# Masked query copies of an attention kernel divided between GpSimd and VectorE

## The chip, the cores and the metric

The kernel runs on one core of a Trainium2 chip. The metric is device time in microseconds (us) of one execution. The engines are named as the profile names them: PE (TensorE; PEld its weight loads), DVE (VectorE), ACT (ScalarE), POOL (GpSimd), SP (SyncE, which issues the loads and stores here). SBUF and PSUM are the two on-chip memories; DVE and ACT read both, POOL works on SBUF here.

## What is computed

For 2048 samples of 40 fields with 64 features, four heads of 32:

```python
q = (einsum('bfe,oe->bfo', x, Wq) + bq).reshape(B, F, H, D)
k = (einsum('bfe,oe->bfo', x, Wk) + bk).reshape(B, F, H, D)
v = (einsum('bfe,oe->bfo', x, Wv) + bv).reshape(B, F, H, D)
att = softmax(einsum('bfhd,bghd->bhfg', q, k) / sqrt(64), axis=-1)
out = einsum('bhfg,bghd->bfhd', att, v).reshape(B, F, H * D)
y = relu(out + einsum('bfe,oe->bfo', x, Wr) + br)
```

## The kernel before

The 2048 samples are done in 256 steps of 8 samples (320 tokens). The steps are pipelined by hand: each engine has one loop over n, and in the loop's group n it works on several steps at once. Engines meet only through counting semaphores, and each engine runs its own instructions in the order in which they are written.

PE, group n: queries and keys of step n (L386, L390, into the two halves of the PSUM tile `o_bank`), scores of step n-1 (L406, into `s_buf`), attention times values of step n-3 (L475, into `o_bank` again), the shift of the scores by their maxima of step n-2 (L452), values and residual of step n (L422 to L438, into `vr_bank`). Since `o_bank` is shared, L386 of step n waits until DVE has divided the result of step n-4 (semaphore `att_ready` at n - 3), and L475 waits until ACT and DVE have copied queries and keys out (`copied`).

DVE, group n: combine and split the maxima of step n-2 (L331, L332, L336, out `m_split`), copy the keys of step n out of PSUM (L320, `kT`), reduce the scores of step n-1 to maxima (L325), and for step n-3 the reciprocal of the sums (L341) and the division (L347, out `y_att`).

ACT, group n: copy the queries of step n out of PSUM (L231, `q_flat`), values and residual (L258), swap maxima (L244), exponentials (L251), relu (L238).

POOL, group n: for step n-2 the diagonal matrices that PE's shift multiplies with (L183, `m_diag`, waits for `m_split`), for step n the masked copies of the queries (L199, `q_bd`), and for step n-4 the sum with the residual (L191, `y_sum`).

The masked copies are needed because 64 rows of `q_flat` hold a pair of heads. `q_bd[:, step, sample, s]` is a copy of the queries in which the rows of the pair's other head are multiplied by 0 and those of head s by 1, so that one matmul of 64 rows gives the scores of both heads, 80 columns. Copy s is one `tensor_scalar` of 128 x 320 fp32 elements, from contiguous `q_flat` in SBUF to `q_bd` in SBUF in 8 rows of 40 elements 80 apart, with a per-partition factor from `consts`. POOL makes both, one after the other. `q_ready` counts them: PE waits for two per step ahead of L390, and ACT before it writes `q_flat`'s buffer again, two steps on.

Of the kernel before, what the change touches and what calls it, by code (L numbers as in the profile page):

```python
# [6 lines left out]
ALU = mybir.AluOpType  # L7
# [27 lines left out]
def attention_kernel(nc, xT_in, w_in, bias_in, vr_bias_in, const_in, out):  # L35
# [3 lines left out]
    with ExitStack() as ctx:  # L39
# [3 lines left out]
        def sem(name):  # L43
            return ctx.enter_context(nc.semaphore(name))
# [47 lines left out]
        qk_made = sem("qk_made")  # L92
        copied = sem("copied")
        q_ready = sem("q_ready")
        scores_made = sem("scores_made")
        vr_made = sem("vr_made")
        vr_ready = sem("vr_ready")
# [24 lines left out]
        def before(n, limit):  # L122
            return n < limit
# [53 lines left out]
        @block.gpsimd  # L177
        def _(pool):
            def diagonals(n, place):
                pool.wait_ge(m_ready, 2 * (n + 1))  # L180
                if not before(n, 1):
                    pool.wait_ge(shifted, n)
                pool.tensor_tensor(m_diag[:], m_split[:, place % 2].unsqueeze(2).to_broadcast([P, BLOCKS, QUAD]),  # L183
                                   ident[:].unsqueeze(1).to_broadcast([P, BLOCKS, QUAD]),
                                   ALU.mult).then_inc(diag_ready, 1)

            def add_residual(n, place):
                pool.wait_ge(att_ready, n + 1)
                if not before(n, 3):
                    pool.wait_ge(y_ready, n - 2)  # L190
                pool.tensor_tensor(y_sum[:, n % 3].rearrange("r (a d) -> r a d", d=DIM), rv[:, place % 4, RESIDUAL * HEADS:(RESIDUAL + SLOTS) * HEADS, 0:DIM],  # L191
                                   y_att[:, place % 2].rearrange("r (a d) -> r a d", d=DIM),
                                   ALU.add).then_inc(sum_ready, 1)

            def query_columns(n, place):
                pool.wait_ge(copied, 2 * (n + 1))

                for s in range(2):
                    pool.tensor_scalar(q_bd[:, place % 4, :, s], q_flat[:, place % 2].rearrange("d (b f) -> d b f", f=FIELDS),  # L199
                                       consts[:, C_HEAD + s:C_HEAD + s + 1], 1.0, ALU.mult, ALU.mult).then_inc(q_ready, 1)  # L200

            def group(n, place):
                if not before(n, 2):
                    diagonals(n - 2, place + 6)
                query_columns(n, place)
                if not before(n, 4):
                    add_residual(n - 4, place + 4)

            pool.wait_ge(prepared, PREPARED)
            pool.wait_ge(set_up, SET_UP)  # L210
            run(group)
            for n in range(STEPS, STEPS + 4):
                if exists(n - 2):
                    diagonals(n - 2, n - 2)
                add_residual(n - 4, n - 4)

        @block.scalar
        def _(act):
            act.dma_start(consts[:], const_in).then_inc(loaded, 16)
            act.dma_start(vr_bias[:], vr_bias_in.to_broadcast([P, 2, OUT])).then_inc(loaded, 16)  # L220
            act.dma_start(biases[:], bias_in).then_inc(loaded, 16)
            act.wait_ge(loaded, LOADS)
            for i in range(4):
                nc.scalar.copy(rv[:, i, :, DIM:VW],
                               consts[:, C_REAL:C_REAL + 1].unsqueeze(2).to_broadcast([P, 2 * SLOTS * HEADS, 1])).then_inc(prepared, 1)

            def queries(n, place):
                act.wait_ge(qk_made, n + 1)
                if not before(n, 2):
                    act.wait_ge(q_ready, 2 * (n - 1))  # L230
                nc.scalar.activation(q_flat[:, place % 2], o_bank[:, 0, 0:TOK], ACT.Identity,  # L231
                                     bias=biases[:, 0:1]).then_inc(copied, 1)

            def relu(n, place):
                if not before(n, 4):
                    act.wait_ge(y_stored[place % 4], 32 * (turn_of(n, place, 4) - 1))
                act.wait_ge(sum_ready, n + 1)
                nc.scalar.activation(y_rows[:, place % 4], y_sum[:, n % 3], ACT.Relu).then_inc(y_ready, 1)  # L238

            def swap_maxima(n, place):  # L240
                act.wait_ge(m_parted, n + 1)
                for g in range(0, P // QUAD, 2):
                    to, of = QUAD * g, QUAD * (g + 1)
                    nc.scalar.copy(m_swap[to:to + QUAD, place % 2], m_part[place % 2][of:of + QUAD]).then_inc(m_swapped, 1)  # L244

            def exponentials(n, place):
                act.wait_ge(shifted, n + 1)
                if not before(n, 2):

                    act.wait_ge(o_made, n - 1)  # L250
                nc.scalar.activation(pT[:, place % 2], s_buf[place % 2][:, :, 0:TOK], ACT.Exp,  # L251
                                     scale=SCALE).then_inc(p_ready, 1)

            def values_and_residual(n, place):
                act.wait_ge(vr_made, n + 1)
                if not before(n, 4):
                    act.wait_ge(sum_ready, n - 3)
                nc.scalar.activation(rv[:, place % 4, :, 0:DIM],  # L258
                                     vr_bank[:].rearrange("k t (a d) -> k (t a) d", d=DIM),
                                     ACT.Copy).then_inc(vr_ready, 1)  # L260

            act.wait_ge(prepared, PREPARED)

            def group(n, place):
                queries(n, place)
                if not before(n, 1):
                    values_and_residual(n - 1, place + 7)
                if not before(n, 1):
                    swap_maxima(n - 1, place + 7)
                if not before(n, 2):  # L270
                    exponentials(n - 2, place + 6)
                if not before(n, 5):
                    relu(n - 5, place + 3)

            run(group)
            for n in range(STEPS, STEPS + 5):
                if exists(n - 1):
                    values_and_residual(n - 1, n - 1)
                    swap_maxima(n - 1, n - 1)
                if exists(n - 2):  # L280
                    exponentials(n - 2, n - 2)
                relu(n - 5, n - 5)

        @block.vector
        def _(dve):
# [32 lines left out]
            def keys(n, place):  # L318
                dve.wait_ge(qk_made, n + 1)
                nc.vector.tensor_scalar(kT[:, place % 4], o_bank[:, 1, 0:TOK], biases[:, 1:2], None,  # L320
                                        ALU.add).then_inc(copied, 1)

            def max_of_quadrants(n, place):
                dve.wait_ge(scores_made, n + 1)
                nc.vector.tensor_reduce(m_part[place % 2].rearrange("k (t b) -> k t b", t=2),  # L325
                                        s_buf[place % 2][:, :, 0:TOK].rearrange("k t (b c) -> k t b c", c=QUAD),
                                        AX.X, ALU.max, apply_transpose=True).then_inc(m_parted, 1)
# [24 lines left out]
            def group(n, place):  # L352
                if not before(n, 2):
                    max_of_keys(n - 2, place + 6)
                keys(n, place)
                if not before(n, 1):
                    max_of_quadrants(n - 1, place + 7)
                if not before(n, 3):
                    normalise(n - 3, place + 5)
                    divide(n - 3, place + 5)  # L360
# [11 lines left out]
        def _(pe):  # L372
# [5 lines left out]
            def queries_and_keys(n, place):  # L378
                if n == 0:
                    pe.wait_ge(x_loaded[0], 32)  # L380
                elif before(n, LAG + 1):
                    pe.wait_ge(copied, 2 * n)
                else:

                    pe.wait_ge(att_ready, n - LAG)
                nc.tensor.matmul(o_bank[:, 0, 0:TOK], w_cols[0:HALF, 0], tokens(place, 0), start=True, stop=True)  # L386
                if n > 0:

                    pe.wait_ge(q_ready, 2 * n)
                nc.tensor.matmul(o_bank[:, 1, 0:TOK], w_cols[HALF:P, 0], tokens(place, HALF),  # L390
                                 start=True, stop=True).then_inc(qk_made, 1)

            def scores(n, place):
# [2 lines left out]
                if not before(n, 2):  # L396
                    pe.wait_ge(p_ready, n - 1)
                if not exists(n + 1):
                    pe.wait_ge(q_ready, 2 * (n + 1))
                for slot in range(SLOTS):  # L400
                    for member in range(MEMBERS):
                        b = MEMBERS * slot + member
# [145 lines left out]
```

## Time and profile before

| | before |
|---|---|
| median of 3 runs | 927.33 us (925.72 to 928.43) |
| the profiled execution, whole | 923.84 us |
| span of its instructions | 921.1 us |
| granted TensorE clock, mean | 0.996 |
| PE busy | 892.3 us (97%) |
| POOL busy | 872.1 us (95%) |
| ACT busy | 770.6 us (84%) |
| DVE busy | 726.7 us (79%) |

The terms of the prediction are durations from the one profiled execution. The 2.7 us between its time and its span are start and end. Busy times are sums over a span whose steady part is 256 like steps; what bounds a step is read from the order of instructions in one step and from who waits for whom.

### The profile page before, as it was taken

The page shows a single profiled execution, that of the slowest core. Times are in us where ns is not written, and L with a number is a line of the kernel's source. Part 1 is how long each engine was busy: PE and PEld are TensorE (multiplying, and loading weights), DVE is VectorE, ACT ScalarE, POOL GpSimd, SP SyncE. Part 2 cuts the span into 40 slices and gives each one's busy share as a digit, 9 for nine tenths or more (in the row PEclk, how much of TensorE's full clock was granted, in tenths as well). Part 3 has the DMA queues.
Part 4 walks back from the last instruction along what each step waited for, and adds up shares of the span by engine and source line. Part 5 has one row for each costly group of instructions (what it writes and reads, how often), then busy time and mean ns, then how long its engine had stood idle before and what let it go on. Part 6 is the DMA issues. An engine that isn't in the chain of part 4 may idle for free.

```text
span 921.1 us, 67888 instructions
## 1 busy us (share of the span) xinstructions
PE 892.3 (97%) x30208; PEld 626.7 (68%) x30208; DVE 726.7 (79%) x2066; ACT 770.6 (84%) x1541; POOL 872.1 (95%) x1028
## 2 busy tenths in 40 slices
PE   6999999999999999999999999999999999999996
PEld 4667666767666776676666667666667766767664
DVE  5878777878787877888887878787878887878785
ACT  4888888888888888888888888888888888888886
POOL 3999999999999999999999999999999999999997
PEclk9999999999999999999999999999999999999998
DMA  4333333333333333333333333333333333333321
GB/s 120 97 110 117 113 105 110 115 107 112 118 112 107 116 111 111 111 117 109 115 112 105 110 111 111 112 112 112 117 111 112 112 120 108 115 110 112 111 83 67
DMA packets 67429, 101.20 MB, mean 110 GB/s; under 512 B 13632, under 2 KB 46656, under 8 KB 67136
## 3 DMA queue, kind: packets, MB, share of 16 engines
q1 hardware_dynamic: 66704, 96.72, 34.7%
q8 instruction: 235, 3.85, 1.8%
q14 instruction: 58, 0.48, 0.2%
q10 hardware_dynamic: 432, 0.15, 0.1%
HBM read 54.88 MB, written 41.94 MB: 105 GB/s over the span
## 4 chain that ended last, share of the span: by engine, by line
PE 93%; POOL 3%; issue 2%; DVE 1%; DMA 0%; ACT 0%; POOLq 0%; ACTq 0%
PE vr_bank L422 24%; PE o_bank L475 22%; PE s_buf L406 19%; PE o_bank L386 15%; PE s_buf L452 7%; PE vr_bank L433 6%; POOL y_sum L191 1%; POOL m_diag L183 1%; POOL q_bd L199 1%; PE o_bank L390 0%; DMA biases<-bias_in 0%; ACT y_rows L238 0%; POOLq L39 0%; DVE s_buf L325 0%; PE vr_bank L438 0%
## 5 line engine op out<-in xcount | busy, mean ns | idle before, releaser
L183 POOL TENSOR_TENSOR m_diag<-m_split,ident 128x640 bf16<-128x640 bf16 x256 | 323.1, 1262 | 32.2 <-DVE m_split L336 30.1
L191 POOL TENSOR_TENSOR y_sum<-rv,y_att 128x512 f32<-128x512 f32 x256 | 303.9, 1187 | 1.9 <-DVE y_att L347 1.9
L199 POOL TENSOR_SCALAR q_bd<-q_flat,consts 128x320 f32<-128x320 f32 x512 | 267.6, 537 | 11.2 <-DVE kT L320 11.1
L422 PE MATMUL vr_bank<-w_cols,xT 64*128 64x128 f32 (+1 forms) x3072 | 269.0, 308 | 0.1
L258 ACT ACTIVATE rv<-vr_bank 128x1024 f32<-128x1024 f32 x256 | 260.4, 1017 | 0.1
L325 DVE TRANSPOSE_TENSOR_REDUCE s_buf<-s_buf 128x20 f32<-128x640 f32 x256 | 221.6, 866 | 47.8 <-PE s_buf L406 47.7
L475 PE MATMUL o_bank<-rv,pT 64*40 64x33 f32 x16384 | 229.6, 202 | 12.1 <-issue 8.4
L406 PEld LDWEIGHTS s_buf<-q_bd,kT 64*40 64x40 f32 x8192 | 151.5, 113 | 116.2 <-issue 115.1
L475 PEld LDWEIGHTS o_bank<-rv,pT 64*40 64x40 f32 x16384 | 192.9, 117 | 54.4 <-issue 17.9
L320 DVE TENSOR_SCALAR kT<-o_bank,biases 128x320 f32<-128x320 f32 x256 | 140.9, 550 | 89.1 <-PE o_bank L390 89.0
L406 PE MATMUL s_buf<-q_bd,kT 64*40 64x80 f32 x8192 | 200.5, 233 | 1.4 <-issue 1.1
L422 PEld LDWEIGHTS vr_bank<-w_cols,xT 64*128 64x128 f32 x3072 | 195.2, 190 | 0.2 <-issue 0.2
L231 ACT ACTIVATE q_flat<-o_bank,biases 128x320 f32<-128x320 f32 x256 | 135.1, 528 | 71.5 <-PE o_bank L390 66.9
L386 PE MATMUL o_bank<-xT,w_cols 64*128 64x320 f32 x512 | 186.8, 445 | 5.7 <-DMA xT<-xT_in 5.7
L251 ACT ACTIVATE pT<-s_buf 128x640 f32<-128x640 f32 x256 | 180.4, 705 | 14.1 <-PE s_buf L452 8.0
L390 PE MATMUL o_bank<-xT,w_cols 64*128 64x320 f32 x512 | 187.5, 446 | 0.0
L347 DVE TENSOR_TENSOR y_att<-o_bank,r_sum 128x512 f32<-128x512 f32 x256 | 177.0, 691 | 9.2 <-DVE r_sum L341 0.3
L238 ACT ACTIVATE y_rows<-y_sum 128x512 f32<-128x512 f32 x256 | 159.1, 622 | 2.5 <-POOL y_sum L191 2.4
L244 ACT COPY m_swap<-s_buf 32x20 f32<-32x20 f32 x512 | 85.9, 168 | 55.5 <-DVE s_buf L325 49.4
L452 PE MATMUL s_buf<-m_diag,pick 64*40 64x320 bf16 x1024 | 114.9, 297 | 2.0 <-POOL m_diag L183 1.6
L386 PEld LDWEIGHTS o_bank<-xT,w_cols 64*128 64x128 f32 x512 | 76.6, 186 | 45.7 <-DVE y_att L347 35.4
L336 DVE TENSOR_TENSOR m_split<-s_buf,m_split 32x20 bf16<-32x20 f32 x512 | 88.5, 173 | 16.6
(31 smaller groups left out, 466.0 us busy)
## 6 DMA issues: line engine op xcount, KB each, us to landing
xT<-xT_in SPq DMA_DIRECT2D x512, 104.0 KB, 2.7
y<-y_rows SPq DMA_DIRECT2D x512, 80.0 KB
w_cols<-w_in SPq DMA_DIRECT2D x1, 192.0 KB, 2.6
vr_bias<-vr_bias_in ACTq DMA_DIRECT2D x1, 128.0 KB, 3.3
consts<-consts_in ACTq DMA_DIRECT2D x1, 20.0 KB, 2.4
biases<-bias_in ACTq DMA_DIRECT2D x1, 1.0 KB, 3.8
```

The costliest lines, as they stand in the source:

```text
L183: pool.tensor_tensor(m_diag[:], m_split[:, place % 2].unsqueeze(2).to_broadcast([P, BLOCKS, QUAD]), ident[:].unsqueeze(1).to_broadcast([P, ...
L191: pool.tensor_tensor(y_sum[:, n % 3].rearrange("r (a d) -> r a d", d=DIM), rv[:, place % 4, RESIDUAL * HEADS:(RESIDUAL + SLOTS) * HEADS, 0 ...
L199: pool.tensor_scalar(q_bd[:, place % 4, :, s], q_flat[:, place % 2].rearrange("d (b f) -> d b f", f=FIELDS), consts[:, C_HEAD + s:C_HEAD + ...
L251: nc.scalar.activation(pT[:, place % 2], s_buf[place % 2][:, :, 0:TOK], ACT.Exp, scale=SCALE).then_inc(p_ready, 1)
L258: nc.scalar.activation(rv[:, place % 4, :, 0:DIM], vr_bank[:].rearrange("k t (a d) -> k (t a) d", d=DIM), ACT.Copy).then_inc(vr_ready, 1)
L325: nc.vector.tensor_reduce(m_part[place % 2].rearrange("k (t b) -> k t b", t=2), s_buf[place % 2][:, :, 0:TOK].rearrange("k t (b c) -> k t ...
L386: nc.tensor.matmul(o_bank[:, 0, 0:TOK], w_cols[0:HALF, 0], tokens(place, 0), start=True, stop=True)
L390: nc.tensor.matmul(o_bank[:, 1, 0:TOK], w_cols[HALF:P, 0], tokens(place, HALF), start=True, stop=True).then_inc(qk_made, 1)
L406: mm = nc.tensor.matmul(s_buf[place % 2][HALF * member:HALF * member + FIELDS, t, 2 * FIELDS * slot:2 * FIELDS * (slot + 1)], kT[rows, pla ...
L422: return nc.tensor.matmul(blocks(half, first, step)[:, 0:count], xT[rows, place % 8, PAIR * pair:PAIR * pair + P], w_cols[rows, 1:1 + coun ...
L452: mm = nc.tensor.matmul(s_buf[place % 2][HALF * member:HALF * member + FIELDS, t, 0:TOK], pick[rows, member, 0:FIELDS], m_diag[rows, t * ( ...
L475: mm = nc.tensor.matmul(o_part[HALF * g:HALF * g + FIELDS, c, idx * HEADS + h], pT[HALF * member:HALF * (member + 1), place % 2, h // 2, a ...
```

## The change

In each step POOL writes the copy of the first head only (s = 0); the copy of the second head (s = 1) becomes a DVE instruction of the same form, written behind the keys' copy L320 and ahead of the maxima L325. DVE waits for `copied` (the queries by ACT and the keys by itself) ahead of it, and counts it on a semaphore of its own, `q_second`. PE waits for `q_second` in the first steps and in the last; in between it is covered by `att_ready`, which the same engine raises later. ACT's wait before it overwrites `q_flat` now counts POOL's copies alone.

```diff
+        q_second = sem("q_second")
...
             def query_columns(n, place):
                 pool.wait_ge(copied, 2 * (n + 1))
 
-                for s in range(2):
-                    pool.tensor_scalar(q_bd[:, place % 4, :, s], q_flat[:, place % 2].rearrange("d (b f) -> d b f", f=FIELDS),
-                                       consts[:, C_HEAD + s:C_HEAD + s + 1], 1.0, ALU.mult, ALU.mult).then_inc(q_ready, 1)
+                pool.tensor_scalar(q_bd[:, place % 4, :, 0], q_flat[:, place % 2].rearrange("d (b f) -> d b f", f=FIELDS),
+                                   consts[:, C_HEAD:C_HEAD + 1], 1.0, ALU.mult, ALU.mult).then_inc(q_ready, 1)
...
-                    act.wait_ge(q_ready, 2 * (n - 1))
+                    act.wait_ge(q_ready, n - 1)
...
+            def query_columns(n, place):
+                dve.wait_ge(copied, 2 * (n + 1))
+                nc.vector.tensor_scalar(q_bd[:, place % 4, :, 1], q_flat[:, place % 2].rearrange("d (b f) -> d b f", f=FIELDS),
+                                        consts[:, C_HEAD + 1:C_HEAD + 2], 1.0, ALU.mult, ALU.mult).then_inc(q_second, 1)
+
...
                 keys(n, place)
+                query_columns(n, place)
                 if not before(n, 1):
                     max_of_quadrants(n - 1, place + 7)
...
                     pe.wait_ge(copied, 2 * n)
+                    pe.wait_ge(q_second, n)
...
-                    pe.wait_ge(q_ready, 2 * n)
+                    pe.wait_ge(q_ready, n)
...
-                    pe.wait_ge(q_ready, 2 * (n + 1))
+                    pe.wait_ge(q_ready, n + 1)
+                    pe.wait_ge(q_second, n + 1)
```

## Rows read from the trace of the kernel before

**Rows 1.** The page: the span and each engine's busy time

```profile
span 921.1 us, 67888 instructions
...
PE 892.3 (97%) x30208; PEld 626.7 (68%) x30208; DVE 726.7 (79%) x2066; ACT 770.6 (84%) x1541; POOL 872.1 (95%) x1028
```

**Rows 2.** Waits: who waited for whom, us in total, times, longest us

```profile
DVE s_buf L325 <- PE s_buf L406: 47.7, 255, 0.8
...
PEld o_bank L386 <- DVE y_att L347: 35.4, 214, 0.3
...
POOL m_diag L183 <- DVE m_split L336: 30.1, 91, 1.6
...
PEld s_buf L452 <- POOL m_diag L183: 1.9, 2, 1.0
...
PE s_buf L452 <- POOL m_diag L183: 1.6, 2, 0.9
```

**Rows 3.** Timeline of a short step: start us, us, engine, line, [idle before it]

```profile
433.64 0.45 PE L386 MATMUL o_bank<-xT,w_cols 64*128 64x320 f32 x1
...
434.16 1.26 POOL L183 TENSOR_TENSOR m_diag<-m_split,ident 128x640 bf16<-128x640 bf16 x1
...
434.41 0.53 ACT L231 ACTIVATE q_flat<-o_bank,biases 128x320 f32<-128x320 f32 x1
434.41 0.55 DVE L320 TENSOR_SCALAR kT<-o_bank,biases 128x320 f32<-128x320 f32 x1 [0.33 <-PE o_bank L390]
...
435.13 0.87 DVE L325 TRANSPOSE_TENSOR_REDUCE s_buf<-s_buf 128x20 f32<-128x640 f32 x1 [0.16 <-PE s_buf L406]
435.40 1.04 POOL L199 TENSOR_SCALAR q_bd<-q_flat,consts 128x320 f32<-128x320 f32 x2
...
435.90 0.26 DVE L341 RECIPROCAL r_sum<-o_bank 128x16 f32<-128x16 f32 x1
...
436.19 0.69 DVE L347 TENSOR_TENSOR y_att<-o_bank,r_sum 128x512 f32<-128x512 f32 x1
436.40 1.19 POOL L191 TENSOR_TENSOR y_sum<-rv,y_att 128x512 f32<-128x512 f32 x1
...
436.94 0.18 PEld L386 LDWEIGHTS o_bank<-xT,w_cols 64*128 64x128 f32 x1 [0.15 <-DVE y_att L347]
...
437.03 0.45 PE L386 MATMUL o_bank<-xT,w_cols 64*128 64x320 f32 x1
...
437.09 0.38 DVE L336 TENSOR_TENSOR m_split<-s_buf,m_split 32x20 bf16<-32x20 f32 x2
...
437.55 1.26 POOL L183 TENSOR_TENSOR m_diag<-m_split,ident 128x640 bf16<-128x640 bf16 x1
...
437.80 0.55 DVE L320 TENSOR_SCALAR kT<-o_bank,biases 128x320 f32<-128x320 f32 x1 [0.33 <-PE o_bank L390]
```

**Rows 4.** Timeline of a long step, same columns

```profile
457.96 0.44 PE L386 MATMUL o_bank<-xT,w_cols 64*128 64x320 f32 x1
...
458.47 1.26 POOL L183 TENSOR_TENSOR m_diag<-m_split,ident 128x640 bf16<-128x640 bf16 x1 [0.23 <-DVE m_split L336]
...
460.48 0.26 DVE L341 RECIPROCAL r_sum<-o_bank 128x16 f32<-128x16 f32 x1 [0.18 <-PE o_bank L475]
...
461.59 0.46 PE L386 MATMUL o_bank<-xT,w_cols 64*128 64x320 f32 x1
```

**Rows 5.** Line L320: count, ns min/median/max, first and last start

```profile
L320 DVE TENSOR_SCALAR kT<-o_bank,biases x256: 546/550/553, 8.4 to 904.9; 128x320 f32<-128x320 f32 x128
```

**Rows 6.** Groups by line and form: single instructions of the set-up, busy us, mean ns

```profile
L293 DVE TENSOR_TENSOR out_bias<-vr_bias 128x128 f32<-128x128 f32 x1 | 0.3, 293 | 1.9 <-DMA biases<-bias_in 1.9
...
L295 DVE CAST bias_high<-out_bias 128x128 bf16<-128x128 f32 x1 | 0.2, 226 | 0.0
...
L311 DVE CAST ident<-consts 128x32 bf16<-128x32 f32 x1 | 0.2, 176 | 0.0
```

**Rows 7.** Timeline of POOL at the start: its first instruction on data

```profile
9.21 1.04 POOL L199 TENSOR_SCALAR q_bd<-q_flat,consts 128x320 f32<-128x320 f32 x2 [8.77 <-DVE kT L320]
```

## The prediction

> **What bounds the kernel now.** I read the page first: PE is busy 97% of the span and POOL 95%, DVE only 79% [rows 1]. That looks like PE and POOL being the limits and DVE having room, which is the case for moving work from POOL to DVE. The waits are read next, and they say something else: of 255 steps, in 214 PE's first weight load of a step (L386) is released by DVE's division L347, while PE waited for POOL's `m_diag` twice, for 1.9 and 1.6 us in sum [rows 2]. So the third view is the timeline of one short step. Taking PE's L386 at 433.64 as zero: DVE copies the keys from 0.77 to 1.32, waits 0.16 for PE's scores, reduces from 1.49 to 2.36, takes the reciprocal from 2.26, divides from 2.55 to 3.24, PE loads the next step's weights at 3.30 and multiplies at 3.39 [rows 3]. From there DVE waits for PE's keys, and the ring closes. Length 3.39 us. Of this ring DVE's own instructions are all but the stretch from the division's end to the next L320 (0.92 us, in which L331 to L336 run) and the 0.16.
>
> POOL's ring is as long: from `m_diag` to `m_diag` 434.16 to 437.55, again 3.39 us, in pieces of 1.24, 1.00 (both copies) and 1.15 us, without a gap [rows 3]. But POOL does not set the step: in the short step `m_diag` starts 0.08 us after `m_split` ends (437.09 + 0.38 = 437.47), and in the long step too it is `m_split` that ends POOL's wait, at 0.51 us after L386 against 0.52 in the short one [rows 3, 4]. `m_diag` stands at this place whether POOL had been idle or not.
>
> Not all steps are short. L320 starts at 8.4 for the first and at 904.9 for the last step: 896.5 / 255 = 3.516 us each [rows 5], 0.126 over 3.39, 32 us in all. The long steps (3.63 in the example) have their delay in the attention matmuls: L341 starts at 2.52 after L386 instead of 2.26, waiting for L475 [rows 3, 4]. POOL's waits count them: 91, with 30.1 us [rows 2], 0.33 each. This matters below, since a longer DVE part hides such delays.
>
> **The change part by part.** *POOL loses one copy of two*: 1.00 / 2 = 0.50 us per step, 128 us in all. Gain on the path: nothing, since `m_diag` starts by `m_split`. An upper bound is the 3.5 us that PE waited for it [rows 2]. The first head's copy keeps its place at 435.40 and ends 0.5 earlier than the pair did; PE needs it only at 437.03 (L386 and L390 of the next step).
>
> *DVE gains a copy of 128 x 320 fp32 per step*, in SBUF on both sides; no such instruction is in the trace. Its duration by the nearest rows: `kT` of the same size and form, but from PSUM, takes 0.550 us [rows 5]. One element takes DVE 1.04 ns at the single pace (a fp32 `tensor_tensor` of 512 elements 0.69 us, one of 128 elements 0.293 [rows 3, 6]), so that is 0.333 us for 320 elements and 0.217 fixed. The casts from fp32 in SBUF to SBUF take 226 ns for 128 elements and 176 for 32 [rows 6]: 50 ns for 96, 0.52 ns each, so two elements in the time of one, and 0.159 fixed. Copy at the doubled pace: 0.167 + 0.217 = 0.384 us; with the casts' fixed part 0.326; at the single pace 0.550. I take 0.384: same operand kinds as the casts, same per-partition factor as `kT`.
>
> *Where it stands*: behind L320 and ahead of L325. Its new wait is for `copied`; keys and queries end at 434.96 and 434.94 [rows 3], and from the reciprocal's end (436.16) to the division that waits for it is 0.03, so it can start at 435.00. It ends at 435.38. The next instruction without a wait of its own starts some 0.09 before the record's end of the one before (L325 ends at 436.00, L341 starts at 435.90). L325 then starts at 435.29 instead of 435.13: the idle 0.16 takes a part, and 0.16 to 0.17 is left. Queued behind are L325, L341 and L347; for L325 ACT's swap waits, for L347 PE's L386. All of them move by this d, and so does the ring: step 3.39 + d. ACT's instructions behind L325 shift with it and keep their phase to PE. Moving work into DVE's idle time is no gain here: the other idle stretch (0.33 ahead of L320) is on the far side of the ring and can't be filled from here.
>
> *What d costs in all*: 256 d, less what the long steps had anyway. With d above 0.33 nearly all of the 32 us go under; with d = 0.17, 91 x 0.17 = 15 us. Undisturbed copy: 923.84 + 43.5 - 15 = 952 us (with 0.326: d = 0.11, 942 us; at the single pace: d = 0.33, 923.84 + 84 - 29 = 979 us).
>
> *The disturbed copy.* No DVE instruction of the doubled pace ran beside POOL in the trace: the casts ran before POOL's first work at 9.21 [rows 7], and in a step each DVE instruction has an operand in PSUM. The copy wants to start at 435.00, and POOL is in the middle of `m_diag`, 434.16 to 435.40 [rows 3]. If the two can't run together, the copy is held by 0.40 us in every step, since `m_diag` hangs on `m_split` and so keeps its distance to DVE's own ring; POOL's lighter load doesn't move it. Price: at the least only the streaming is left after 435.40 (end 435.57, L325 at 435.48, d = 0.35), at the most the copy begins as a whole at 435.42 (end 435.80, L325 at 435.71, d = 0.58). I take d = 0.50, nearer the upper end, because the rows show fixed parts exposed wherever an instruction waits for another engine. Sum: 923.84 + 128 - 32 = 1020 us; ends 923.84 + 90 - 31 = 983 and 923.84 + 148 - 32 = 1040 us.
>
> The Trainium skill ("SBUF — State Buffer", Who interferes with whom) says that GpSimd's only port pair into SBUF is VectorE's second one, that it is an exclusive lock held for the whole instruction by whoever starts first, and that an fp32 `tensor_scalar` from SBUF to SBUF is of the kind that takes it. No row here shows that; by it the sum would be the 1020 us of the disturbed copy, without it 952.
>
> **The rivals.** Forecast: held copy, 1020 us, own range 983 to 1040. For it: the doubled pace appears only where both sides are in SBUF, so it may hang on a way into SBUF that DVE has not to itself, and POOL runs through the very moment, in each step. Against it: nothing in the trace shows DVE and POOL disturbing each other; POOL's `m_diag` and DVE's instructions beside it keep their durations.
>
> *Rival 1, undisturbed copy at the doubled pace*: 952 us (942 to 958). For it: constant durations of all DVE rows beside a busy POOL, though none is of this kind.
>
> *Rival 2, undisturbed copy at the single pace*: 979 us. For it: the strided output, which no cast had.
>
> *Rival 3, POOL's next instruction gets in ahead of the copy*: POOL queues its own copy right behind `m_diag`; then DVE is held until 435.90, d = 1.0, 923.84 + 256 - 32 = 1148 us. For it: POOL's instructions follow each other without a gap [rows 3].
>
> *Rival 4, not slower*: DVE's copy fits into the 0.16 us and the load taken from POOL pays. It decides whether L325 starts by 435.13, which needs a copy whose end lets it, about 0.22 us long; then the time is 923.84 us, and with the 3.5 us that PE waits for POOL gone, 920.3 us, 0.4% faster. Against it: the streaming alone is 0.167, and a fixed part under 0.06 appears in no row.
>
> **How the numbers follow.** A measurement of this kernel can tell about 0.3% from no change. Chances: held copy 0.62, rival 1 0.18, rival 2 0.08, rival 3 0.07, rival 4 0.05 (0.02 faster, 0.03 within 0.3%). The first three lie between 942 and 1040 and hold 0.88; the range is theirs, with a little above: 942 to 1045. Slower by over 0.3%: 0.62 + 0.18 + 0.08 + 0.07 = 0.95. The sum is made against the profiled execution, 923.84 us; the median of the runs, 927.33, lies 0.4% above it, so a median of the changed kernel may lie some 3 us above its sum.
>
> **What would show it.** In the changed kernel's profile: L325 waits no longer for PE's L406 (47.7 us before) and L341 no longer for L475, while L386's wait for L347 grows from 0.15 to some 0.6 us per step; POOL's busy time falls by 128 us and its wait for `m_split` rises to some 1.0 us in each step. The new copy's row decides between the cases: its mean is near 0.38 (rival 1), 0.55 (rival 2), or the copy is recorded with the wait, some 0.8 us, or starts late, at `m_diag`'s end (forecast); ending with POOL's own copy it is rival 3. Wrong at the root would be the ring: if L325 moves and the division or PE's L386 doesn't, or if the long steps' delays are added to the longer step instead of hidden in it (then up to 32 us more).

## The result, and the profile after

The changed kernel takes 976.56 us (median of 4 runs, 975.66 to 977.08) against 926.53 us before (4 runs): 1.0544 times as long, 95% interval 1.0509 to 1.058. The profiled execution took 975.66 us, its span is 973.9 us; forecast were 1020 us, with 942 to 1045 as the range.

The page of the changed kernel, its head and its chain that ended last:

```profile
span 973.9 us, 67891 instructions
...
PE 933.7 (96%) x30208; PEld 615.4 (63%) x30208; DVE 840.7 (86%) x2322; ACT 770.3 (79%) x1541; POOL 764.8 (79%) x772
...
DVE 61%; PE 25%; issue 12%; POOL 1%; ACT 0%; DMA 0%; POOLq 0%; ACTq 0%
```

POOL is at 79% instead of 95%, DVE at 86% instead of 79% [rows 1]: the load is spread more evenly, and the kernel is slower. The chain runs through DVE for 61% of the span. In the page of the kernel before, the same line reads:

```profile
PE 93%; POOL 3%; issue 2%; DVE 1%; DMA 0%; ACT 0%; POOLq 0%; ACTq 0%
```

PE was itself busy almost without a break there, so that a chain followed backwards stays on it; that DVE's division released PE's first weight load in 214 of 255 steps shows only in the waits [rows 2]. The waits of the changed kernel (who for whom, us, times, longest us):

```profile
POOL m_diag L184 <- DVE m_split L341: 192.2, 255, 1.9
...
PEld o_bank L393 <- DVE y_att L352: 123.8, 252, 0.6
...
DVE s_buf L330 <- PE s_buf L414: 0.6, 1, 0.6
```

Against [rows 2]: PE's wait for the division (now L352 and L393) has risen from 35.4 to 123.8 us and stands in 252 steps; DVE's 47.7 us of waiting ahead of the maxima (now L330) are gone; POOL waits 192 us for DVE where it waited 30.

One step of the changed kernel in the timeline, which answers to [rows 3] (start us, us, engine, line):

```profile
431.96 1.26 POOL L184 TENSOR_TENSOR m_diag<-m_split,ident 128x640 bf16<-128x640 bf16 x1 [0.74 <-DVE m_split L341]
...
432.21 0.53 ACT L231 ACTIVATE q_flat<-o_bank,biases 128x320 f32<-128x320 f32 x1
432.21 0.55 DVE L320 TENSOR_SCALAR kT<-o_bank,biases 128x320 f32<-128x320 f32 x1 [0.33 <-PE o_bank L397]
...
432.80 0.60 DVE L325 TENSOR_SCALAR q_bd<-q_flat,consts 128x320 f32<-128x320 f32 x1
...
433.20 0.60 POOL L199 TENSOR_SCALAR q_bd<-q_flat,consts 128x320 f32<-128x320 f32 x1
433.33 0.85 DVE L330 TRANSPOSE_TENSOR_REDUCE s_buf<-s_buf 128x20 f32<-128x640 f32 x1
...
434.09 0.21 DVE L346 RECIPROCAL r_sum<-o_bank 128x16 f32<-128x16 f32 x1
...
434.34 0.69 DVE L352 TENSOR_TENSOR y_att<-o_bank,r_sum 128x512 f32<-128x512 f32 x1
...
435.08 0.18 PEld L393 LDWEIGHTS o_bank<-xT,w_cols 64*128 64x128 f32 x1 [0.49 <-DVE y_att L352]
...
435.94 0.55 DVE L320 TENSOR_SCALAR kT<-o_bank,biases 128x320 f32<-128x320 f32 x1 [0.33 <-PE o_bank L397]
```

The copy starts as soon as keys and queries are there, at 432.80, while `m_diag` runs since 431.96. POOL's next instruction starts at 433.20; the copy's record ends 0.20 after that, at 433.40. The ring by its pieces, in us:

| from start to start | before [rows 3] | after |
|---|---|---|
| kT to the maxima (L325, now L330) | 0.72 | 1.12 |
| maxima to reciprocal | 0.77 | 0.76 |
| reciprocal to division | 0.29 | 0.25 |
| division to PE's load of the next step | 0.75 | 0.74 |
| that load to the next kT | 0.86 | 0.86 |
| step | 3.39 | 3.73 |

The same instruction when POOL isn't in its way stands in the start of the same execution (timeline, 5 to 20 us):

```profile
8.83 0.39 DVE L325 TENSOR_SCALAR q_bd<-q_flat,consts 128x320 f32<-128x320 f32 x1
...
12.28 0.39 DVE L325 TENSOR_SCALAR q_bd<-q_flat,consts 128x320 f32<-128x320 f32 x1
12.34 0.73 POOL L199 TENSOR_SCALAR q_bd<-q_flat,consts 128x320 f32<-128x320 f32 x1 [2.73 <-DVE kT L320]
...
14.62 1.26 POOL L184 TENSOR_TENSOR m_diag<-m_split,ident 128x640 bf16<-128x640 bf16 x1 [1.56 <-DVE m_split L341]
...
15.53 0.53 DVE L325 TENSOR_SCALAR q_bd<-q_flat,consts 128x320 f32<-128x320 f32 x1
...
18.02 1.26 POOL L184 TENSOR_TENSOR m_diag<-m_split,ident 128x640 bf16<-128x640 bf16 x1 [1.56 <-DVE m_split L341]
...
18.78 0.68 DVE L325 TENSOR_SCALAR q_bd<-q_flat,consts 128x320 f32<-128x320 f32 x1
```

0.39 us in the first two steps, before any `m_diag`. Then 0.53 and 0.68: in both the record ends 1.44 us after the start of `m_diag` (15.53 + 0.53 - 14.62; 18.78 + 0.68 - 18.02), as in the step above (433.40 - 431.96), whenever the copy had started (0.91 and 0.76 after `m_diag` there, 0.84 in the later step). So it is in all 254 steps in which the copy starts during `m_diag`: ends 1.439 to 1.445 us after `m_diag`'s start. That is 0.20 after the start of POOL's next instruction and 0.18 after `m_diag`'s recorded end. It is the end of `m_diag` that sets the copy's end, not a slower pace.

### The profile page after: what moved, and what is told of

Read it like the earlier page. It is cut to its first block, busy times and chain, and to the rows that moved or that the text cites. A ratio compares the mean times of both kernels' runs of the same rounds, so it can differ in the third digit from the quotient of the medians.

```text
span 973.9 us, 67891 instructions
## 1 busy us (share of the span) xinstructions
PE 933.7 (96%) x30208; PEld 615.4 (63%) x30208; DVE 840.7 (86%) x2322; ACT 770.3 (79%) x1541; POOL 764.8 (79%) x772
## 4 chain that ended last, share of the span: by engine, by line
DVE 61%; PE 25%; issue 12%; POOL 1%; ACT 0%; DMA 0%; POOLq 0%; ACTq 0%
PE o_bank L393 21%; DVE y_att L352 17%; DVE q_bd L325 15%; DVE kT L320 14%; DVE s_buf L330 8%; DVE r_sum L346 6%; PE vr_bank L430 1%; PE o_bank L397 1%; PE o_bank L483 1%; PE s_buf L414 1%; DMA biases<-bias_in 0%; POOL y_sum L192 0%; PE vr_bank L441 0%; PE s_buf L460 0%; POOL m_diag L184 0%
## 5 line engine op out<-in xcount | busy, mean ns | idle before, releaser
L393 PE MATMUL o_bank<-xT,w_cols 64*128 64x320 f32 x512 | 206.2, 483 | 28.8 <-DMA xT<-xT_in 5.6
L414 PEld LDWEIGHTS s_buf<-q_bd,kT 64*40 64x40 f32 x8192 | 149.3, 113 | 113.0 <-issue 111.7
L330 DVE TRANSPOSE_TENSOR_REDUCE s_buf<-s_buf 128x20 f32<-128x640 f32 x256 | 218.1, 852 | 0.6 <-PE s_buf L414 0.6
L320 DVE TENSOR_SCALAR kT<-o_bank,biases 128x320 f32<-128x320 f32 x256 | 140.9, 550 | 86.6 <-PE o_bank L397 86.6
L483 PE MATMUL o_bank<-rv,pT 64*40 64x33 f32 x16384 | 211.3, 201 | 1.9 <-ACT pT L251 0.9
L483 PEld LDWEIGHTS o_bank<-rv,pT 64*40 64x40 f32 x16384 | 182.1, 118 | 38.8 <-issue 1.7
L397 PE MATMUL o_bank<-xT,w_cols 64*128 64x320 f32 x512 | 206.2, 483 | 0.0
L414 PE MATMUL s_buf<-q_bd,kT 64*40 64x80 f32 x8192 | 195.9, 233 | 0.4 <-ACT pT L251 0.4
L352 DVE TENSOR_TENSOR y_att<-o_bank,r_sum 128x512 f32<-128x512 f32 x256 | 177.0, 691 | 8.7
L199 POOL TENSOR_SCALAR q_bd<-q_flat,consts 128x320 f32<-128x320 f32 x256 | 154.5, 604 | 11.3 <-DVE kT L320 11.3
L325 DVE TENSOR_SCALAR q_bd<-q_flat,consts 128x320 f32<-128x320 f32 x256 | 154.3, 603 | 9.1
L393 PEld LDWEIGHTS o_bank<-xT,w_cols 64*128 64x128 f32 x512 | 76.1, 185 | 129.6 <-DVE y_att L352 123.8
L460 PE MATMUL s_buf<-m_diag,pick 64*40 64x320 bf16 x1024 | 112.8, 297 | 1.2 <-POOL m_diag L184 1.2
```

The lines of the kernel that those rows point to most:

```text
L325: nc.vector.tensor_scalar(q_bd[:, place % 4, :, 1], q_flat[:, place % 2].rearrange("d (b f) -> d b f", f=FIELDS), consts[:, C_HEAD + 1:C_H ...
L352: nc.vector.tensor_tensor(y_att[:, place % 2].rearrange("r (c a d) -> r c a d", c=2, d=DIM), o_part[:, :, :, 0:DIM], r_sum[:].unsqueeze(3) ...
L414: mm = nc.tensor.matmul(s_buf[place % 2][HALF * member:HALF * member + FIELDS, t, 2 * FIELDS * slot:2 * FIELDS * (slot + 1)], kT[rows, pla ...
L483: mm = nc.tensor.matmul(o_part[HALF * g:HALF * g + FIELDS, c, idx * HEADS + h], pT[HALF * member:HALF * (member + 1), place % 2, h // 2, a ...
```

## The experiments

Two theories stood after this. Hold: a copy of this kind can't run while a POOL instruction runs, it waits for that one's end, and the ring passes the delay on; POOL's relief is worth nothing. Load: beside a busy POOL such a copy simply takes 0.60 us. The first four kernels ran on one chip (before: 925.13 us, 13 runs), the other three on another (before: 925.25 us, 7 runs).

**1. POOL's relief alone.**

```diff
+            nc.vector.memset(q_bd[:, :, :, 1].rearrange("d i b f -> d (i b) f"), 0.0).then_inc(prepared, 1)
...
                 keys(n, place)
-                query_columns(n, place)
...
```

> GpSimd writes the first head's copy, nobody writes the second (its half of q_bd is filled with zeros once at the start, so that part of the computation is left out). This is the changed kernel's lighter GpSimd without VectorE's copy. Theory of the ring (PE keys, DVE kT, L325, reciprocal, division, PE again sets the step): short steps stay at 3.39 us, the time is within 0.5% of before, some 921 to 929 us with 1 us for the zeros, and GpSimd waits for m_split about 0.5 us in every step. Rival (GpSimd's 3.39 us of work per step was a bound as well): short steps fall below 3.36 us and the time below 915 us.

Measured: 927.77 us, ratio 1.0013 (0.9967 to 1.006). Waits of this kernel, and the keys' copy of two short steps in a row:

```profile
POOL m_diag L184 <- DVE m_split L337: 166.0, 256, 2.1
```

```profile
432.80 0.55 DVE L321 TENSOR_SCALAR kT<-o_bank,biases 128x320 f32<-128x320 f32 x1 [0.33 <-PE o_bank L391]
...
436.19 0.55 DVE L321 TENSOR_SCALAR kT<-o_bank,biases 128x320 f32<-128x320 f32 x1 [0.33 <-PE o_bank L391]
```

POOL is idle for 0.65 us in each step on average, the short step is 3.39 us as before, and the time is that of before, 0.3% below to 0.6% above by the interval. The relief buys nothing that can be measured even when it costs nothing. So POOL did not set the step before the change, though its three instructions filled the short step of 3.39 us to the last hundredth [rows 3].

**2. POOL out of the way at that moment.**

```diff
-                pool.tensor_tensor(m_diag[:], m_split[:, place % 2].unsqueeze(2).to_broadcast([P, BLOCKS, QUAD]),
-                                   ident[:].unsqueeze(1).to_broadcast([P, BLOCKS, QUAD]),
+                pool.tensor_tensor(m_diag[:, 0:2], m_split[:, place % 2, 0:2].unsqueeze(2).to_broadcast([P, 2, QUAD]),
+                                   ident[:].unsqueeze(1).to_broadcast([P, 2, QUAD]),
...
+            nc.vector.memset(m_diag[:].rearrange("r b i -> r (b i)"), 0.0).then_inc(prepared, 1)
...
```

> The changed kernel, but GpSimd's m_diag instruction writes 2 of its 20 blocks (the other 18 are zeros from the start; the shift by the maxima is left out for them), so that GpSimd is idle when VectorE's copy wants to start. Theory of the hold (the copy can't run while a GpSimd instruction runs): the copy's record falls from 0.604 to 0.385 us, as in the first two steps, the step from 3.73 to 3.50 to 3.56 us, the time to 935 to 952 us. Rival (in the steady state the copy takes 0.60 us whatever GpSimd does, by load on SBUF or the strided output): the copy stays at 0.55 to 0.60 and the time at 965 to 977 us.

Measured: 938.71 us, ratio 1.0107 (1.0027 to 1.0188). The two copies' lines (ns min/median/max, first and last start), and both in one step of the timeline:

```profile
L326 DVE TENSOR_SCALAR q_bd<-q_flat,consts x256: 385/387/389, 9.0 to 922.6; 128x320 f32<-128x320 f32 x128
L199 POOL TENSOR_SCALAR q_bd<-q_flat,consts x256: 603/722/727, 9.1 to 922.7; 128x320 f32<-128x320 f32 x128
```

```profile
438.90 0.39 DVE L326 TENSOR_SCALAR q_bd<-q_flat,consts 128x320 f32<-128x320 f32 x1
...
438.97 0.72 POOL L199 TENSOR_SCALAR q_bd<-q_flat,consts 128x320 f32<-128x320 f32 x1 [0.61 <-DVE kT L321]
439.20 0.86 DVE L331 TRANSPOSE_TENSOR_REDUCE s_buf<-s_buf 128x20 f32<-128x640 f32 x1
```

The copy is 0.387 us in all 256 steps, though POOL's own copy runs beside it for 0.32 us, so the load theory falls. Now POOL's copy pays: it starts 0.07 us after DVE's and takes 0.72 us, against 0.53 in experiment 1, where DVE has no copy. The hold works both ways, and who starts first is not touched: DVE's record has no hundredth more.

**3. The same work at the single pace.**

```diff
+                pool.tensor_scalar(q_bd[:, place % 4, 7, 1], q_flat[:, place % 2, 7 * FIELDS:8 * FIELDS],
+                                   consts[:, C_HEAD + 1:C_HEAD + 2], 1.0, ALU.mult, ALU.mult).then_inc(q_ready, 1)
...
-                nc.vector.tensor_scalar(q_bd[:, place % 4, :, 1], q_flat[:, place % 2].rearrange("d (b f) -> d b f", f=FIELDS),
+                nc.vector.tensor_scalar(q_bd[:, place % 4, 0:7, 1], q_flat[:, place % 2, 0:7 * FIELDS].rearrange("d (b f) -> d b f", f=FIELDS),
                                         consts[:, C_HEAD + 1:C_HEAD + 2], 1.0, ALU.mult, ALU.mult).then_inc(q_second, 1)
...
```

> The changed kernel, but VectorE copies 7 of the 8 rows of 40 elements in its one instruction, GpSimd the last row in an instruction of its own. The Trainium skill (VectorE: DVE Perf Modes, Mode 2x_2P) wants the outermost dimensions even on both sides or equal; seven rows at the output against 280 contiguous elements at the input miss that. Theory of the hold: the instruction runs at the single pace and is not held by m_diag, 0.217 + 280 x 1.04 ns = 0.51 us against 0.604, L325 starts 1.02 us after kT instead of 1.12, the step is 3.63 us and the time some 950 to 958 us. Rival (slowed by the load on SBUF, whatever the pace): seven eighths of the copy take 0.53 us or more, 965 us or more. If the pace is doubled in spite of the odd count, it is held and the time stays at 970 to 977 us.

Measured: 953.98 us, ratio 1.028 (1.0213 to 1.0347). The copy's line, and a step:

```profile
L327 DVE TENSOR_SCALAR q_bd<-q_flat,consts x256: 503/504/505, 9.1 to 938.7; 128x280 f32<-128x280 f32 x128
```

```profile
438.42 1.26 POOL L184 TENSOR_TENSOR m_diag<-m_split,ident 128x640 bf16<-128x640 bf16 x1 [0.45 <-DVE m_split L343]
...
439.25 0.50 DVE L327 TENSOR_SCALAR q_bd<-q_flat,consts 128x280 f32<-128x280 f32 x1
...
439.65 0.53 POOL L199 TENSOR_SCALAR q_bd<-q_flat,consts 128x320 f32<-128x320 f32 x1
439.67 0.85 DVE L332 TRANSPOSE_TENSOR_REDUCE s_buf<-s_buf 128x20 f32<-128x640 f32 x1
```

280 elements take 0.504 us where 320 took 0.387: 280 x 1.04 ns and 0.213 fixed, the single pace. And this instruction, from SBUF to SBUF like the other, runs through `m_diag` and into POOL's copy without a trace of either: 503 to 505 ns in all steps, and POOL's copy has its 0.53 us. The slower instruction is through earlier (L332 starts 1.00 us after kT, against 1.12), and the kernel is 23 us faster than the change at hand. Not all of that is the pace: DVE also copies one row less, 40 x 1.04 ns = 0.042 us per step or some 11 us, so that by this estimate a whole copy at the single pace would take some 965 us, 12 less than the change. That wasn't run. The hold goes with the doubled pace: of these two copies with the same operands, the one at that pace was held, the other was not. The Trainium skill ("VectorE: DVE Perf Modes", Mode 2x_2P) had named the shape that falls out of it, an odd outermost count at the output against an even one at the input (280 elements in one run, as the row prints it); the row's duration agrees.

**4. The copy at another place.**

```diff
+                    act.wait_ge(q_second, n - 1)
...
                 keys(n, place)
-                query_columns(n, place)
...
                     divide(n - 3, place + 5)
+                query_columns(n, place)
...
-                    pe.wait_ge(q_second, n)
...
-                    pe.wait_ge(q_second, n + 1)
+                pe.wait_ge(q_second, n + 1)
...
```

> The changed kernel with VectorE's copy moved behind the division L347 of the same loop turn, off the stretch between the keys and PE's next L386; PE's scores wait for it, and ACT before it writes q_flat again. Theory of the hold: GpSimd is then in y_sum, from 2.27 to 3.42 us after L386; the copy, free to start at 3.15, ends some 0.20 after y_sum, at 3.62, recorded at 0.45 to 0.50 us. The ring through the division is as short as before, but L331 to L336 come 0.3 to 0.4 us later, m_diag ends at 2.1 to 2.2 instead of 1.78, and PE's shift waits 0.1 to 0.2 us for it: step 3.45 to 3.60 us, 935 to 960 us. Rival (the copy costs its 0.6 us wherever it stands): step 3.7, 970 us.

Measured: 991.28 us, ratio 1.0679 (1.0609 to 1.0749): slower than the change itself, and outside what I expected. A step:

```profile
439.77 1.26 POOL L184 TENSOR_TENSOR m_diag<-m_split,ident 128x640 bf16<-128x640 bf16 x1 [0.85 <-DVE m_split L342]
...
441.01 0.54 POOL L199 TENSOR_SCALAR q_bd<-q_flat,consts 128x320 f32<-128x320 f32 x1
...
441.51 1.19 POOL L192 TENSOR_TENSOR y_sum<-rv,y_att 128x512 f32<-128x512 f32 x1
441.51 0.69 DVE L353 TENSOR_TENSOR y_att<-o_bank,r_sum 128x512 f32<-128x512 f32 x1
...
442.12 0.76 DVE L326 TENSOR_SCALAR q_bd<-q_flat,consts 128x320 f32<-128x320 f32 x1
...
443.08 0.38 DVE L342 TENSOR_TENSOR m_split<-s_buf,m_split 32x20 bf16<-32x20 f32 x2
...
443.49 0.55 DVE L321 TENSOR_SCALAR kT<-o_bank,biases 128x320 f32<-128x320 f32 x1
443.54 1.26 POOL L184 TENSOR_TENSOR m_diag<-m_split,ident 128x640 bf16<-128x640 bf16 x1 [0.84 <-DVE m_split L342]
```

The hold is there as expected, now by `y_sum`: the copy ends at 442.88, 1.37 after the start of `y_sum`, which is 0.18 after that one's recorded end (1.19), as it was 0.18 after the recorded end of `m_diag`. What I had wrong is that I left `y_sum` where it had been. The held copy delays L342, L342 delays `m_diag`, and that, through POOL's own order, delays the next `y_sum`, which holds the next copy for longer: 0.76 us in place of 0.45 to 0.50. This is a ring of its own, and it closes by the rows: `m_diag` to `q_bd` 1.24, to `y_sum` 0.50, to the copy's end 1.37, to the next `m_diag` 0.66, in sum 3.77 us, the step. DVE comes late to kT (L321, which no longer waits for PE), and attention waits for kT. The forecast assumed POOL's timetable fixed; it hangs on DVE, and here POOL's work, worth nothing before, is part of what sets the step.

**5. Both copies on DVE.**

```diff
-                pool.tensor_scalar(q_bd[:, place % 4, :, 0], q_flat[:, place % 2].rearrange("d (b f) -> d b f", f=FIELDS),
-                                   consts[:, C_HEAD:C_HEAD + 1], 1.0, ALU.mult, ALU.mult).then_inc(q_ready, 1)
...
-                nc.vector.tensor_scalar(q_bd[:, place % 4, :, 1], q_flat[:, place % 2].rearrange("d (b f) -> d b f", f=FIELDS),
-                                        consts[:, C_HEAD + 1:C_HEAD + 2], 1.0, ALU.mult, ALU.mult).then_inc(q_second, 1)
+                for s in range(2):
+                    nc.vector.tensor_scalar(q_bd[:, place % 4, :, s], q_flat[:, place % 2].rearrange("d (b f) -> d b f", f=FIELDS),
+                                            consts[:, C_HEAD + s:C_HEAD + s + 1], 1.0, ALU.mult, ALU.mult).then_inc(q_second, 1)
...
```

> The changed kernel with both heads' copies on VectorE, one behind the other at the same place, and none on GpSimd, whose next instruction behind m_diag is then y_sum. Theory of the hold: the first copy ends 1.44 us after m_diag's start, as in the changed kernel; the second costs its undisturbed 0.30 us (0.385 less the overlap of 0.085), if VectorE keeps its turn: step 3.73 + 0.30 = 4.03 us, 1048 to 1056 us. If y_sum gets in between the two, the second copy is held by 1.15 us more: step about 5.1 us, some 1300 us. Rival (a copy beside GpSimd costs 0.60 us each): step 4.25 us, 1105 us.

Measured: 1284.61 us, ratio 1.3872 (1.3789 to 1.3954). POOL and DVE in one step:

```profile
438.72 1.26 POOL L184 TENSOR_TENSOR m_diag<-m_split,ident 128x640 bf16<-128x640 bf16 x1 [2.47 <-DVE m_split L339]
439.94 1.26 POOL L192 TENSOR_TENSOR y_sum<-rv,y_att 128x512 f32<-128x512 f32 x1
```

```profile
439.56 1.82 DVE L323 TENSOR_SCALAR q_bd<-q_flat,consts 128x320 f32<-128x320 f32 x2
441.30 0.85 DVE L328 TRANSPOSE_TENSOR_REDUCE s_buf<-s_buf 128x20 f32<-128x640 f32 x1
```

The two copies, 0.69 us if nothing disturbs them (0.387 + 0.30), take 1.82. `y_sum` starts at 439.94, 0.14 ahead of the second copy's recorded start, and gets in between the two, so the second waits for all of it and is recorded with 1.30 us: the step is 4.95 us (kT, L317, starts at 438.97 and 443.92), 0.92 above the 4.03 without it and near the 5.1 written down for this case, which had put 1.15 on it. This is the mechanism of rival 3 of the prediction, at another instruction: a copy that waits while POOL's next instruction runs.

**6. The holding instruction in two pieces.**

```diff
-                pool.tensor_tensor(m_diag[:], m_split[:, place % 2].unsqueeze(2).to_broadcast([P, BLOCKS, QUAD]),
-                                   ident[:].unsqueeze(1).to_broadcast([P, BLOCKS, QUAD]),
-                                   ALU.mult).then_inc(diag_ready, 1)
+                for low, high in ((0, 14), (14, BLOCKS)):
+                    pool.tensor_tensor(m_diag[:, low:high], m_split[:, place % 2, low:high].unsqueeze(2).to_broadcast([P, high - low, QUAD]),
+                                       ident[:].unsqueeze(1).to_broadcast([P, high - low, QUAD]),
+                                       ALU.mult).then_inc(diag_ready, 1)
...
```

> The changed kernel with GpSimd's m_diag written by two instructions, 14 blocks and then 6, the first ending about 0.08 us after VectorE's copy wants to start. Theory of the hold by one whole instruction, after which the waiting VectorE comes first: the copy is recorded near 0.39 to 0.45 us, the second piece waits for it, m_diag is complete some 0.4 us later than in one piece and PE's shift becomes the late one: step 3.55 to 3.68 us, 940 to 965 us. If GpSimd's second piece comes first instead, the copy ends after it, at 2.1 us after L386: step 3.85 to 3.95 us, 1005 to 1030 us.

Measured: 968.05 us, ratio 1.0456 (1.0404 to 1.0508), between the two cases. Two steps in a row:

```profile
435.81 1.59 POOL L185 TENSOR_TENSOR m_diag<-m_split,ident 128x448 bf16<-128x448 bf16 x2 [0.75 <-DVE m_split L342]
...
436.64 0.39 DVE L326 TENSOR_SCALAR q_bd<-q_flat,consts 128x320 f32<-128x320 f32 x1
...
439.32 1.41 POOL L185 TENSOR_TENSOR m_diag<-m_split,ident 128x448 bf16<-128x448 bf16 x2 [0.26 <-DVE m_split L342]
...
440.17 0.73 DVE L326 TENSOR_SCALAR q_bd<-q_flat,consts 128x320 f32<-128x320 f32 x1
```

The second pieces by themselves:

```profile
436.70 0.69 POOL L185 TENSOR_TENSOR m_diag<-m_split,ident 128x192 bf16<-128x192 bf16 x1
...
440.21 0.51 POOL L185 TENSOR_TENSOR m_diag<-m_split,ident 128x192 bf16<-128x192 bf16 x1
```

In one step the copy comes ahead of the second piece (0.39 us, the piece 0.69), in the next behind it (0.73, the piece 0.51), and so on in turn in most of the steps: the copy starts 0.83 after the first piece in the one and 0.85 in the other, 0.06 and 0.04 ahead of the second piece's recorded start, and 0.02 us decide. The hold lasts for one POOL instruction, and what gets in at its end is a matter of hundredths.

**7. DVE's part of the change alone.** The edit against the kernel before:

```diff
+        q_spare = sb("q_spare", [P, 4, GROUP, 2, FIELDS])
...
+            def query_columns(n, place):
+                dve.wait_ge(copied, 2 * (n + 1))
+                nc.vector.tensor_scalar(q_spare[:, place % 4, :, 1], q_flat[:, place % 2].rearrange("d (b f) -> d b f", f=FIELDS),
+                                        consts[:, C_HEAD + 1:C_HEAD + 2], 1.0, ALU.mult, ALU.mult).then_inc(q_second, 1)
+
...
                 keys(n, place)
+                query_columns(n, place)
...
```

> GpSimd makes both copies as in the kernel before, and VectorE's copy is added at the place of the changed kernel, into a spare tile that nobody reads. It has VectorE's part of the change alone, with GpSimd's load as before. Theory (the hold by m_diag and the ring explain all, GpSimd's relief nothing): the copy ends 1.44 us after m_diag's start, step 3.73 us, 972 to 980 us. Rival (GpSimd's relief had given something back): GpSimd's 3.39 us and the time for which the copy holds it, 0.07 to 0.2, make it the bound of a step or delay y_sum: 985 us or more.

Measured: 977.6 us, ratio 1.0556 (1.0503 to 1.0608), the change's own 976.56 within the spread. The whole loss is DVE's copy, and the relief of POOL is worth nothing beside it: with experiment 1 that makes the change.

## Why the prediction was right, and where its size was off

**The ring, not POOL's load, sets the step**: right. Experiment 1 takes POOL's work away for nothing, experiment 7 leaves it all, and the times are those of before and after. PE, busy for 97%, is the other candidate for what bounded the kernel before, and no run made PE's work lighter or the ring shorter. The rows speak for the ring: PE's load of the next step starts 0.75 us after the division's start in the short step before and 0.74 after, as soon as the division lets it. But it had waited only 0.15 us for it, so PE was close behind. A shorter ring wasn't tried.

**The copy's own cost**: 0.384 us was worked out, 0.387 measured where nothing holds it (experiment 2); the doubled pace, taken from two casts of the set-up [rows 6], was right.

**The hold by `m_diag`**: right, and as the rows stood only a bet, at 0.62. The copy started at 0.04 us after kT's end and was held in 254 of 256 steps, all but the first two. The Trainium skill ("SBUF — State Buffer", Who interferes with whom) puts it down to a port pair that the two engines share and that the first to start keeps for its whole instruction; experiments 2, 3, 5 and 6 agree: mutual (0.72 against 0.53 us), for whole instructions (the copy's end 0.18 us after the recorded end of `m_diag` or `y_sum`), first come first served (`y_sum` in experiment 5) as far as recorded starts tell it, which in experiment 6 were 0.04 us out, and absent at the single pace (503 to 505 ns). That it is a port is the page's word; the runs show the behaviour.

**Its price, d = 0.50 us per step**: this term was mis-sized. Measured is 0.34 (3.73 - 3.39). Two things are in the difference. The copy ended 0.20 us after POOL's next instruction started, not the 0.38 of a whole copy: what was left after the hold was nearly the 0.167 of streaming, the low end of the bounds, as if the fixed part had run during the hold. I had taken the upper half because fixed parts show after a wait for a semaphore; here the instruction had started and waited inside. That moves the maxima by 0.40 instead of 0.50. And of the 0.40, 0.06 came back behind it, 0.04 of it between reciprocal and division (0.29 to 0.25, the reciprocal's record 0.21 instead of 0.26), which the sum had passed on in full. In the traces this goes with PE's attention matmuls, whose result the reciprocal reads: before, its record is 0.26 us in the 238 steps in which it starts within 0.08 us of the end of the last of them, and 0.22 in the other 18; after, it starts 0.46 us behind them and takes 0.21. Whether it is a wait for them inside the record wasn't tried. Experiments 2 and 3 show the same: by the medians of their short steps the maxima come 0.17 and 0.29 us later, and the step is 0.13 and 0.24 longer.

**Long steps hidden**: right. Kernel after, line L320:

```profile
L320 DVE TENSOR_SCALAR kT<-o_bank,biases x256: 544/550/552, 8.2 to 958.0; 128x320 f32<-128x320 f32 x128
```

(958.0 - 8.2) / 255 = 3.725 us per step, the length of the single step above: no long ones are left over. The sum with the measured d is 923.84 + 256 x 0.34 - 32 = 979 us against 975.66 measured; from the starts of L320, 255 x (3.725 - 3.516) = 53 us and 977 us.

**What it should show**: the maxima's wait for PE gone, yes; the reciprocal's wait for L475 (now L483) down from 22.3 to 2.8 us, yes; PE's wait for the division 0.49 us per step, 0.6 expected, as d was smaller. POOL's busy time fell by 107 us, not 128, mainly since its remaining copy takes 0.604 us where the unheld one of experiment 1 takes 0.532: DVE's copy, which ends 0.20 us after POOL's has started, holds it. Its idle time per step is 0.75 instead of 1.0 us for that reason and the shorter step.

**Rivals.** Rival 2, single pace and no hold, would have given nearly the measured time, 979 us; the time alone doesn't tell it from the hold. The copy's record does: 0.55 us was its mark, measured is 0.604 with an end tied to `m_diag` (0.8 was expected for the hold, with d too large), and experiment 3 shows what the single pace looks like. Rival 1 is experiment 2 in kind: 938.7 us with the copy free, where I had said 952 for it, again because d was passed on in full. Rival 3 did not come: in the 254 steps the waiting copy was always ahead of POOL's own copy. Rival 4 and the upper bound on POOL's relief used 3.5 us, which counts two waits twice: the rows of the weight load and of the matmul are the same two waits (at 16.5 and 912.4 us), so the bound was 1.9 us.

No version here beats the kernel before. By experiment 1 none that only takes one of these copies off POOL should: the interval there leaves at most 0.3% to be had from it.

## What to carry to other kernels

An engine that is busy for 95% of the span need not set the time: before work is moved off it, find the ring of waits that a step closes, and ask whether the busy engine starts by itself or by another's signal. Work moved into another engine's idle time is free only if the idle stretch lies where the work is put and is long enough; here 0.16 us stood against 0.39. And a DVE copy at the doubled pace beside a busy POOL costs the rest of the POOL instruction in progress: look up in the timeline what POOL is doing at that moment, and consider the single pace. With one row of eight left to POOL it was faster here by 23 us, about half of it by the estimate from the pace.

## What the runs showed of the hardware that I had not expected

- A held copy is recorded from its start, so the hold sits inside its duration (0.604 instead of 0.387, up to 1.30 us in experiment 5) and not in the idle time ahead of it; a view of the waits alone shows nothing. Its record ends 0.18 us after the recorded end of the instruction that held it, less than half of a whole copy.
- At the end of a hold by `m_diag` the waiting copy came first in all 254 steps: it had started 0.40 us ahead of POOL's next instruction. Between two copies of DVE, back to back, POOL's `y_sum` got in, which had started 0.14 ahead of the second (experiment 5: 0.92 us more per step). Where the copy was recorded only 0.04 to 0.06 ahead, either came first (experiment 6).
- One row of 40 elements less, and the pace falls to the single one with 0.504 us in place of 0.387, and the instruction is finished earlier all the same: 1.34 us after `m_diag`'s start instead of 1.44.
